# Output tiles of the last batch but one begun a slot later, the gather of batch 0 three beats later, W1's last splits five beats sooner

## What is computed

```python
qkv = x @ W_attn + b_attn
scores = einsum('bhki,bhqi->bhkq', k, q) / sqrt(32)      # causal mask, softmax over axis 2
attn = softmax(where(mask, scores, -10000), axis=2)
out = einsum('bhkq,bhkl->bhql', attn, v) @ W_out + b_out
x = layernorm(x + out)
score = x @ w_router                                      # top 512 of 1024 tokens of each batch
h = gelu(selected @ W1 + b1); processed = h @ W2 + b2     # 512 -> 2048 -> 512
x = layernorm(x.at[top_idx].add(sigmoid(score) * processed))
```

## Time and profile before

| | |
|---|---|
| runs | 2494.77, 2498.66, 2497.37 us; median 2497.37 |
| the profiled execution | 2497.64 us, span 2495.8 us |
| granted TensorE clock, mean of the span | 0.993 |
| TensorE busy | 2437.9 us, 98% |
| VectorE busy | 1677.7 us, 67% |
| GpSimd busy | 1566.2 us, 63% |
| ScalarE busy | 1227.0 us, 49% |

### The profile page before, as it was taken

How to read it: one execution, slowest core, us unless ns; L and a number is a source line. 1 busy time by engine, 2 the same in 40 slices (tenths; PEclk the granted TensorE clock), 3 DMA queues, 4 the chain that set the end, 5 groups by cost and what they waited for, 6 DMA issues and landing times.

```text
span 2495.8 us, 40908 instructions
## 1 busy us (share of the span) xinstructions
PE 2437.9 (98%) x14104; PEld 1798.0 (72%) x14104; DVE 1677.7 (67%) x4384; ACT 1227.0 (49%) x2211; POOL 1566.2 (63%) x1481
## 2 busy tenths in 40 slices
PE   8999999999999999999999999998999999999997
PEld 6666676777677767676767667763788888888886
DVE  6767778778777777777888787775755544553533
ACT  3665566666566666666666666666531111111110
POOL 2877888788877888877888888885323132221311
PEclk9999999999999999999999999998999999999999
DMA  4233445335344444534434354343421011010100
GB/s 178 95 128 117 161 138 199 129 124 187 136 146 162 145 145 141 175 133 166 157 129 161 125 180 145 128 162 97 169 64 43 19 34 33 26 34 26 32 20 17
DMA packets 167649, 287.72 MB, mean 115 GB/s; under 512 B 23258, under 2 KB 58138, under 8 KB 166172
## 3 DMA queue, kind: packets, MB, share of 16 engines
q1 hardware_dynamic: 160276, 268.26, 31.1%
q0 software_dynamic: 7168, 16.85, 2.1%
HBM read 117.23 MB, written 65.11 MB: 73 GB/s over the span
## 4 chain that ended last, share of the span: by engine, by line
PE 83%; POOL 11%; DVE 2%; issue 1%; ACT 1%; DMA 0%; SPq 0%; POOLq 0%; DVEq 0%; ACTq 0%
PE PS L1623 14%; PE PS L1602 14%; PE PS L1464 11%; POOL Pa L902 10%; PE PS L1549 10%; PE PS L1515 9%; PE PS L1567 9%; PE PS L1472 8%; PE PS L1477 6%; PE PS L1484 2%; POOL Pm L858 1%; PE PS L1439 1%; PE PS L1583 0%; DVE nm L1130 0%; DVE xTl L1223 0%
## 5 line engine op out<-in xcount | busy, mean ns | idle before, releaser
L902 POOL TENSOR_TENSOR Pa<-Pa,Pm 128x512 f32<-128x512 f32 (+1 forms) x602 | 751.9, 1271 | 129.3 <-ACT Pm L1012 106.7
L1549 PE MATMUL PS<-Qp,Kp 128*128 128x512 f32 (+3 forms) x1536 | 491.0, 355 | 8.7 <-ACT Pm L1012 4.1
L1515 PE MATMUL PS<-Kp,Qp 128*128 128x512 f32 (+3 forms) x1536 | 485.3, 351 | 6.6 <-DVE nm L1130 5.5
L1012 ACT ACTIVATE Pm<-PS 128x512 f32<-128x512 f32 (+1 forms) x643 | 358.3, 568 | 243.7 <-PE PS L1549 194.0
L1130 DVE TENSOR_REDUCE nm<-PS 128x1 f32<-128x512 f32 x512 | 344.7, 687 | 157.2 <-PE PS L1515 156.9
L902 POOL TENSOR_TENSOR Pa<-Pa,P 128x512 f32<-128x512 f32 (+1 forms) x297 | 371.9, 1274 | 64.7 <-ACT P L1012 53.6
L1515 PEld LDWEIGHTS PS<-Kp,Qp 128*128 128x128 f32 x1536 | 276.2, 189 | 105.4 <-issue 41.6
L974 ACT ACTIVATE G<-PS,b1c 128x512 f32<-128x512 f32 x128 | 88.2, 689 | 536.5 <-PE PS L1602 520.3
L1549 PEld LDWEIGHTS PS<-Qp,Kp 128*128 128x128 f32 x1536 | 274.8, 189 | 93.5 <-ACT Pa L1012 29.0
L1138 DVE CUSTOM_DVE_ANT_0 PS<-PS,maskA 128x384 f32<-128x384 f32 (+3 forms) x512 | 246.3, 509 | 121.9 <-PE PS L1515 119.9
L1623 PE MATMUL PS<-W2h,Gs 128*128 128x512 f32 x1024 | 316.6, 390 | 1.1 <-DVE W2l L1228 1.1
(11 more groups left out here) (154 smaller groups left out, 4261.2 us busy)
## 6 DMA issues: line engine op xcount, KB each, us to landing
Qp<-nat SPq DMA_DIRECT2D x192, 256.0 KB, 2.5
Kp<-nat SPq DMA_DIRECT2D x192, 256.0 KB, 2.9
o_s<-Of SPq DMA_DIRECT2D x64, 256.0 KB, 2.1
xb<-in_x SPq DMA_DIRECT2D x64, 256.0 KB, 3.4
Ot<-o_s SPq DMA_DIRECT2D x64, 256.0 KB, 3.0
h_s<-hs SPq DMA_DIRECT2D x64, 256.0 KB, 2.1
out<-xb SPq DMA_DIRECT2D x64, 256.0 KB, 2.2
x_raw<-in_xt SPq DMA_DIRECT2D x15, 1024.0 KB, 6.4
```

Of the source, the lines that this page charges most:

```text
L902: e.tensor_tensor(to, to, probs(u, k)[:, h0:h0 + many, 0:w], ALU.add).then_inc(s["padd"], many)
L1012: e.activation(probs(u, k)[:, hh[0]:hh[-1] + 1, 0:w], tile_bank(j)[:, 0:len(hh) * w].rearrange("p (h n) -> p h n", n=w), ACT.Exp).then_inc ...
L1515: ins = e.matmul(to, Qp[:, u % 4, h_, qt * P:qt * P + P], Kp[:, (2 * i + k0 // 512) % 4, h_, 0:w], start=True, stop=True)
L1549: ins = e.matmul(tile_bank(j)[:, x_ * w:x_ * w + w], Kp[:, (2 * i + k // 4) % 4, h_, k % 4 * P:k % 4 * P + P], Qp[:, u % 4, h_, 512 - w:51 ...
```

## The change

Five edits, all of them in the schedule:
- `LATE_TILES`: slot 58 has no output tile. Tiles 48 to 51 stand in slots 59 to 62, one slot later than before. Slot 63 has tiles 52 and 53; 52 was in slot 62, 53 was there. Tiles 54 and 55 stay in slots 64 and 65.
- `earliest`: tile 53 (batch 6, t = 5) begins no sooner than beat 8 of its slot, so that it stands at beats 8 to 11 of slot 63, and tile 52 at beats 0 to 3, where 53 was.
- What hangs on a tile's beat moves with it: its loads, its bias addition, its statistics, normalisation and stores. Tile 53's bias addition now has beat 8 of slot 63 (before, tile 54's had it); tile 54's has beat 13, and tile 55's slot 64, beat 5 (before slot 63, beat 15). The first tile with its roots on GpSimd is 51 and was 52.
- `GATHER` goes from slot 64, beat 2, to slot 64, beat 5.
- The last four splits of W1 stood from slot 64, beat 14, to slot 65, beat 4; they go to slot 64, beats 9 to 15.

```diff
+LATE_SLOT = 8 * (B - 1) + 2
+LATE_TILES = ((), (48,), (49,), (50,), (51,), (52, 53), (54,), (55,))
 LAG = 2
-GATHER = 63 * 16 + 18
+GATHER = 64 * 16 + 5
...
-    o = slot - 10
-    out = [("O", o // 8, o % 8)] if 0 <= o < 8 * (B - 1) else []
+    first = LATE_SLOT - 10
+    tiles = LATE_TILES[slot - LATE_SLOT] if LATE_SLOT <= slot <= U + 1 else (slot - 10,)
+    out = [("O", o // 8, o % 8) for o in tiles if 0 <= o < (8 * (B - 1) if slot >= LATE_SLOT else first)]
...
+    if job[0] == "O" and job[1] == B - 2:
+        return {5: 8}.get(job[2], 0)
...
-        w1_at = [BEATS * (U - 1) + x_ for x_ in (14, 16, 18, 20, 30, 32, 34, 36)]
+        w1_at = [BEATS * (U - 1) + x_ for x_ in (14, 16, 18, 20, 25, 27, 29, 31)]
```

## The result

The changed kernel took 2502.81 us (median of 19 executions, 2500.95 to 2504.81) against 2497.11 for the kernel before beside it (19 executions, 2494.77 to 2500.51): a ratio of 1.0021 with a 95% interval of 1.0015 to 1.0027. It is slower by 5.2 us by the ratio (3.7 to 6.7), by 5.7 between the medians. The profiled execution took 2503.98 with a span of 2502.2, so the span grew by 6.4. In the changed file every line from L370 on is 5 higher: the evacuation L1204 is L1209, the bias addition L909 is L914, the cut L858 is L863, the transpose of the maxima L1522 is L1527, the products with V L1567 are L1572.

The account below looks back on a forecast made before the run. TensorE is busy for 98%, but GpSimd was taken to bound slot 63 and its addition run slots 58 and 59. -0.6 + 4.3 - 2.65 + 1.35 - 0.1 = +2.3 us gave 2499.6; range (8 in 10) 2491.5 to 2504.0.

Parts of the forecast that it names:

- the slower rival: Clock at its lower level when the products with V at 1728.73 start: +3.6 us, 2503.2; chance 0.24.
- The tile that leaves slot 58: Slots 58 and 59: only 0.6 of the tile's 2.72 us comes out, the rest becomes waiting in slot 59.
- sign (1): Slots 58 and 59: GpSimd's additions of unit 57 last as long as before and TensorE waits for them in slot 59.
- the faster rival: TensorE's price decides in slots 58 and 63: -5.7 to -6.5 us, 2491.5; chance 0.15.
- The tile that comes into slot 63: Tile 53's late bias addition holds VectorE, so unit 62's first product with V comes 4.3 us later.
- Sign (2): Slot 63: VectorE idles at L1204 until L909 ends; unit 63's L1522 comes some 4 us later after unit 61's last addition.
- The gather: Moved behind the cut of unit 62's fourth tile: gives back TensorE's 2.65 us wait, with nothing late in its place.
- Sign (3): No wait for the cut L858 ahead of unit 62's last product.
- The splits: Two W1 splits on ScalarE ahead of unit 63's products with V: net +1.35 us, bounds 0 and 2.1.
- sign (4): ScalarE runs without a gap from the products of unit 62 to those of unit 63.
- The transposes: VectorE is free at the transposes, where TensorE waits 1.89 us for hT: 0.1 us back, bounds 0 and 1.89.
- The order of work is the same, so the offset stays: After slot 65 the order of work is unchanged, so the summed offset of +2.3 us remains to the end.

Follow-up runs that it names:

- e2_tiles: Kernel before with only the output tiles moved, gather and W1's splits at their old beats: 2502.68 us against 2498.12, ratio 1.0015.
- e1_gather: Kernel before with only the gather moved three beats later: 2498.28 us against 2498.12, ratio 0.9997.
- e4_no_splits: Changed kernel with W1's last four splits back at their old beats: 2501.66 us against 2498.12 for the kernel before, ratio 1.0011.
- e3_splits: Kernel before with only W1's last four splits five beats sooner: 2501.56 us against 2498.12, ratio 1.0014.
- e6_add_sooner: Changed kernel with tile 53's bias addition at slot 63, beat 5: 2501.14 us against 2497.83 for the kernel before, ratio 1.0015.
- e7_list: Changed kernel with the second list store of each slot pair moved from beat 13 to beat 4: 2500.36 us, one execution.
- e8_gather_repeat: Kernel before with the gather three beats later and unit 63's score matmuls of steps 1 to 3 issued twice: 2495.74 us against 2497.83, ratio 0.9993.
- e5_repeat: Changed kernel with unit 63's score matmuls issued three times (steps 1, 2) and twice (step 3): 2503.55 us against 2497.83 for the kernel before.
- e11_mended: Changed kernel with old splits, bias addition at beat 5, list store at beat 4, unit 63's steps 1 to 3 issued twice: 2494.37 us, ratio 0.9992.
- e9_warm: Kernel before with later gather, unit 63's score matmuls (steps 1 to 3) and some of units 61 and 62 repeated: 2493.1 us against 2497.07, ratio 0.9988.

## Why the prediction was right or wrong, point by point

The direction and the range held: 2502.81 lies between 2491.5 and 2504.0. But the forecast was 2499.6, +2.3 us where +5.2 came, and the range holds only because it reached out to the slower rival's 2503.2. The likeliest outcome, 2492.4 to 2502.4 with a chance of 0.58, was missed by 0.4 us. By its steps:

**The tile that leaves slot 58: -0.6, measured -0.56.** Slots 58 to 60 take 78.85 us for 79.41. GpSimd and TensorE after the change, in order of time:

```profile
1562.39 5.02 POOL L907 TENSOR_TENSOR Pa<-Pa,Pm 128x512 f32<-128x512 f32 x4 [5.09 <-ACT Pm L1017]
...
1593.42 1.28 POOL L914 TENSOR_TENSOR xb<-xb,CB 128x512 f32<-128x512 f32 x1
```

```profile
1593.52 1.07 PE L1489 MATMUL PS<-Pa,ones 128*32 128x512 f32 x8 [0.31 <-POOL Pa L907]
...
1595.39 1.06 PE L1572 MATMUL PS<-Pa,V 128*32 128x512 f32 x8 [0.59 <-issue]
```

The run from 1562.39 to 1593.42 is as long as the one of rows 4 within 0.4 us, and TensorE, with the tile's 2.72 us of matmuls out of its way, waits for it at the column sums and once more behind them, for the cut of unit 58 that ends at 1595.30. That is sign (1), and the faster rival's first half did not come. The waits stand just behind the transpose that ends slot 59 (1592.94), which is why three slots are compared: slots 58 and 59 alone are 1.56 shorter, and slot 60 gives 1.00 of it back.

**The tile that comes into slot 63: +4.3, measured +4.59** (e2_tiles: +4.57). VectorE, then GpSimd, after the change, in order of time:

```profile
1703.56 0.69 DVE L1209 TENSOR_TENSOR xb<-PS,xb 128x512 f32<-128x512 f32 x1 [8.19 <-POOL xb L914]
...
1705.56 0.17 DVE L1343 BATCH_NORM_AGGREGATE lnmv<-lnst 128x2 f32<-128x6 f32 x1
```

```profile
1702.19 1.27 POOL L914 TENSOR_TENSOR xb<-xb,CB 128x512 f32<-128x512 f32 x1
1705.82 0.19 POOL L872 TENSOR_SCALAR lnrs<-lnmv 128x1 f32<-128x1 f32 x1 [2.36 <-DVE lnmv L1343]
...
1709.10 0.64 POOL L863 TENSOR_SCALAR_AFFINE_SELECT Pa<-Pa 128x512 f32<-128x512 f32 x1
```

VectorE sits idle for 8.19 us for the bias addition, GpSimd 2.36 for the statistics, and the cut ends at 1709.74; the prediction's chain had 1703.6, 1706.1 and 1709.7. From the bias addition to the product it is 7.65 us, worked out as 7.7. Sign (2) is right: the transpose follows the addition's start by 4.30 instead of 0.54. The cut took 0.64, not the 1.62 of rows 6, as the Trainium skill (page "SBUF — State Buffer", section "SBUF: two separate sides") had it for a cut with no VectorE instruction of two inputs beside it. The other 0.3 is GpSimd: it comes to the bias addition only 0.11 us sooner than before, while the slot opens 0.46 sooner.

**The gather: -2.65, measured -2.72** at unit 63's first product (the changed kernel against e2_tiles, in which no moved split lies ahead of that mark; e1_gather -2.61). Nothing is late in its place: the last indirect load ends at 1729.5, the transposes that read it start at 1741.26. Sign (3) is right. But at the block it is worth 3.54 (e4_no_splits against e2_tiles, 55.97 and 59.51), since the half clock behind the old wait went with it. I had that 1.6 for the faster rival alone, and it belonged into the sum by 0.9.

**The splits: +1.35 with bounds 0 and 2.1, measured +1.89** from unit 63's first product to the block (9.06 us in the changed kernel, 7.17 in e4_no_splits). At the block the two are 2.34 apart, but 0.45 of that stands at unit 63's first product already, ahead of every moved split. It is the clock: busy time of each engine from unit 62's first product to unit 63's, in the changed kernel and in e4_no_splits.

```profile
1709.84:1722.51 12.67, 11.92 (x92) 6.40 (x96) 7.56 (x10) 10.36 (x19) 5.83 (x8) 0.91 0.32 100
...
1710.84:1723.07 12.23, 11.48 (x93) 6.31 (x96) 7.57 (x10) 10.37 (x19) 5.83 (x8) 0.95 0.36 104
```

Without the rest of the change the splits give +0.88 at the block. ScalarE in order of time after the change:

```profile
1726.35 1.06 ACT L963 ACTIVATE W1h<-W1r 128x1024 fp32r<-128x1024 f32 x1
...
1728.73 1.09 ACT L963 ACTIVATE W1h<-W1r 128x1024 fp32r<-128x1024 f32 x1
```

Two splits lie ahead of the last exponential, as counted (1.06 and 1.09; with the overlap 0.95 and 0.94 to what follows, 1.89), and ScalarE has no gap from 1722.37 on, sign (4). But ScalarE was the bound there already: once the gather's wait was out, nothing of a split was hidden, and TensorE's waits of 0.93 and 0.75 come with the splits (e3_splits has two of 0.93 there, e1_gather and e4_no_splits none). The 0.45 us of clock is in both terms with opposite sign. Without it the gather gave 3.09 for 2.65 and the splits took 1.89 for 1.35; the two misses cancel by luck, and the offset at the block is 3.30 where I had 3.0.

**The transposes: -0.1, measured 0.** The wait for hT is 1.89 after as before, and in e1_gather too.

**"The order of work is the same, so the offset stays"** is the step that failed. The block took 5.70 for 3.57, +2.13, and the end 14.02 for 12.46, +1.56. -0.56 + 3.30 + 2.13 + 1.56 = 6.4, the growth of the span. The prediction's own sign of being wrong, a half-clock stretch that is longer by over 3 us, is what came: 3.69 us more for the same matmuls. The forecast had put the clock at nothing and left it to the slower rival at a chance of 0.24. Its price, 3.6 for 3.7, was near by luck: not 3.57 doubled, but 2.13 there and 1.56 in a second stretch that it did not have.

Its point of decision was wrong. It was to come true where TensorE's waits before the block are longer than those before 1721.19. In the changed kernel they were 1.10 + 0.93 + 0.75, just over the one of 2.65 in sum and well under it one by one; in e1_gather it came true with a single wait of 1.10. In e2_tiles it did not, although TensorE waits 4.28 us there ahead of the transpose of the maxima (3.56 in the changed kernel) and 2.66 ahead of the cut. What the kernels show is a matter of place. Where the 2.65 us wait stands and the splits come late (before, e2_tiles), the clock falls right behind it, on work that ScalarE slows anyway, and is back for the block. Where gather or splits are moved (after, e1_gather, e3_splits, e4_no_splits, e6_add_sooner, e7_list) it falls on the block, in e3_splits there too, as long as no repeats fill the waits. The Trainium skill (page "TensorE: Matmul & The Clock Gate", section "HAM oscillation — how this bites in real kernels") has idle gaps bring the slow clock; e8_gather_repeat agrees, since filling them kept the clock up. That the longer gap is the worse one the runs don't show: the 2.66 us of e2_tiles cost nothing at the block, the 1.10 us of e1_gather 1.6.

**What stays open.** The end is 12.4 in some kernels (before, e2_tiles, e5_repeat, e6_add_sooner, e8_gather_repeat, e11_mended) and 14.0 in the others, with the same 1.89 us wait ahead of it; I have no rule for which. Where the clock fell in the slower executions of e5_repeat stays open too. And each kernel has one profile (the changed one two), while the clock differs between executions of one kernel. It also falls in places that the change does not touch: in the kernel before it is at 0.66 from 79 to 84 us of the span, with TensorE busy throughout. This is why the marks count for more here than the spans.

Three of the prediction's figures don't follow from its own terms, and none of them decided the outcome. The faster rival's -6.5 would be 2490.9 (2491.5 goes with about -5.9); the upper bound of tile 53's term is 4.3 + 0.45 + 0.97 = 5.7 and not 5.6; and its lower bound of 3.3 is neither 4.3 less the root chain (2.7) nor less the addition (3.0).

## What to carry to other kernels

A wait that is taken out of a stretch with other waits may buy a slow stretch of the clock on the dense work behind it: add to each such gain the price of the next dense block at half clock, from its rows, and look at the granted clock there first. Where TensorE waits for another engine just ahead of dense work, matmuls that are repeated without effect can keep the clock up. In e8_gather_repeat they cost nothing (the block comes at 51.52, without them at 51.75); in e5_repeat the median gained nothing. When work is moved into a slot whose engine is idle, follow the small instructions it brings on the other engines: here 2.7 us of matmuls were free, and what came with them in GpSimd's order cost 4.6, of which the late place of one addition of 1.27 us was 2.7 (e6_add_sooner).

## What the runs showed of the hardware

The clock cost a kernel more than the wait it replaced: the gather's move took out 2.65 us of waiting and 3.26 us at the block, and all of it but 0.1 went again as half clock (5.19 for 3.57, 14.00 for 12.46). Two profiles of the changed kernel, on separate occasions, agree within 0.04 us at each mark. But executions of one kernel can differ: e9_warm's eleven have mean clocks from 0.993 (2498.34 us) to 0.998 (2491.65 us).

A GpSimd instruction on one column is held up beside VectorE as a whole tile is. GpSimd, then VectorE, after the change, in order of time:

```profile
1718.97 1.07 POOL L872 TENSOR_SCALAR lnrs<-lnmv 128x1 f32<-128x1 f32 x1
1720.10 1.08 POOL L873 TENSOR_SCALAR lnrs<-lnmv 128x1 f32<-128x1 f32 x1
...
1742.96 0.19 POOL L872 TENSOR_SCALAR lnrs<-lnmv 128x1 f32<-128x1 f32 x1 [10.75 <-DVE lnmv L1343]
```

```profile
1718.80 2.33 DVE L1233 TENSOR_TENSOR W1l<-W1r,W1h 128x1024 fp32r<-128x1024 f32 x2
```

The 128x1 instruction takes 0.19 us alone and 1.07 beside a run of two splits with two inputs each on VectorE, which take 2.33. The rule of the Trainium skill cited above says this of any GpSimd instruction that reads SBUF, and the trace agrees. The two such instructions of a root chain cost 1.8 us more there.
